# x projected two units ahead, raw token rows in a buffer of their own, expert weights loaded during the last unit, and three shared up-projections at the start of the second stage

## The reference, cut to what matters

```python
def _L0_attn_ref(x, in_proj_w, in_proj_b, conv_w, conv_b, A_log, D, x_proj_w, dt_proj_w, dt_proj_b, out_proj_w, out_proj_b):
    xz = x @ in_proj_w.T + in_proj_b
    x_in, z = jnp.split(xz, 2, axis=-1)
    x_conv = jax.nn.silu(sum((x_pad[:, k:k + L, :] * conv_w[None, None, :, k] for k in range(D_CONV))) + conv_b)
    x_dbl = x_conv @ x_proj_w.T                     # dt_low, B, C
    dt = jax.nn.softplus(dt_low @ dt_proj_w.T + dt_proj_b)
    def step(h, inp):                               # one time step, 512 channels x 16 states
        A_bar = jnp.exp(dtt[..., None] * A)
        B_bar = (A_bar - 1.0) / safe_A * Bt[:, None, :]
        h = A_bar * h + B_bar * xt[..., None]
        return (h, jnp.einsum('bds,bs->bd', h, Ct) + D * xt)
    y = ys * jax.nn.silu(z)
    return y @ out_proj_w.T + out_proj_b
def _L0_ffn_ref(...):                               # 16 experts, top 2, and a shared one
    router_logits = jax.nn.sigmoid(x @ gate_w + gate_b)
    expert_values, expert_indices = jax.lax.top_k(router_logits, k=TOP_K)
    return x + _mlp(x, shared_wg, shared_wu, shared_wd) + expert_weighted
x = _layernorm(x + _L0_attn_ref(...)); x = _layernorm(x + _L0_ffn_ref(...))
```

## Time and profile before

| | |
|---|---|
| median of 3 runs | 2379.16 us (2376.68 to 2380.75) |
| the profiled execution | 2379.85 us, span 2378.0 us |
| first stage, first scan to the barrier | from 56 to 2014.8 us |
| tiles of the experts | 2038.6 to 2280.1 us |
| shared expert and second norm | 2280.1 to 2378.0 us |

### The profile page before, as it was taken

One profiled execution on the slowest core, in us unless ns is written; L12 is line 12 of the kernel. 1 busy time (PEld: TensorE's weight loads), 2 busy tenths in 40 slices (PEclk: granted clock), 3 DMA queues, 4 the chain that ended last, 5 costly groups with the idle time before them and its releaser, 6 DMA issues. The chain is left out here.

```text
span 2378.0 us, 68478 instructions
## 1 busy us (share of the span) xinstructions
PE 2111.4 (89%) x26114; PEld 1270.0 (53%) x26114; DVE 1768.7 (74%) x2992; ACT 1835.2 (77%) x4074; POOL 1772.8 (75%) x1716
## 2 busy tenths in 40 slices
PE   6888989898989898989898989898989878899997
PEld 2454545454555554545455555555545544688864
DVE  2687878787878788787878787878786878555556
ACT  5787888888888879797979797978787875455537
POOL 2688787878686969696969787878787877476654
PEclk8899999999999999999999999999999999899999
DMA  2132333333333323333223232323222333796667
GB/s 92 55 95 89 103 90 95 98 93 93 96 94 93 99 89 96 93 91 92 91 83 99 75 113 79 104 89 100 92 91 93 89 108 98 229 278 213 197 195 265
DMA packets 159218, 269.19 MB, mean 113 GB/s; under 512 B 26536, under 2 KB 74284, under 8 KB 158510
## 3 DMA queue, kind: packets, MB, share of 16 engines
q1 hardware_dynamic: 143294, 220.01, 30.6%
q0 software_dynamic: 15600, 44.79, 5.4%
HBM read 206.27 MB, written 58.45 MB: 111 GB/s over the span
## 5 line engine op out<-in xcount | busy, mean ns | idle before, releaser
L574 POOL TENSOR_TENSOR hc<-h,c_rep 128x512 f32<-128x512 f32 x1024 | 1284.8, 1276 | 369.6 <-DVE h L1129 122.6
L1129 DVE TENSOR_TENSOR_SCAN h<-g_ps,carry,h 128x512 f32<-128x512 f32 x1024 | 1281.5, 1274 | 104.2 <-ACT h L646 79.8
L646 ACT ACTIVATE h<-dt,a_mat 128x512 f32<-128x512 f32 x1024 | 692.0, 712 | 17.4 <-POOL hc L574 16.4
L924 PEld LDWEIGHTS g_ps<-b_steps,x_conv_rows 64*64 64x64 f32 x16384 | 491.5, 137 | 331.4 <-issue 237.5
L924 PE MATMUL g_ps<-b_steps,x_conv_rows 64*64 64x128 f32 x16384 | 569.4, 278 | 74.2 <-DVE h L1129 67.8
L885 PE MATMUL y_ps<-hc,dg_inv 64*64 64x512 f32 x2048 | 525.3, 628 | 23.1 <-POOL hc L574 22.5
L886 PE MATMUL y_ps<-hc,dg_inv 64*64 64x512 f32 x2048 | 523.9, 628 | 0.0
L885 PEld LDWEIGHTS y_ps<-hc,dg_inv 64*64 64x64 f32 x2048 | 141.5, 139 | 261.3 <-issue 168.1
L662 ACT ACTIVATE b_steps<-steps_of,bc_tok 128x64 f32<-128x64 f32 x1024 | 255.9, 341 | 0.0
L1628 POOL DMA_INDIRECT y_planes<-gathered,home x144 | 138.5, 962 | 97.3 <-DVE gathered L2032 74.4
L1120 DVE TENSOR_TENSOR g_ps<-g_ps,minus_u 128x16 f32<-128x16 f32 x512 | 86.8, 170 | 129.8 <-PE g_ps L924 127.2
(11 more groups left out here) (277 smaller groups left out, 2893.1 us busy)
## 6 DMA issues: line engine op xcount, KB each, us to landing
c_rep<-bc_rows SPq DMA_DIRECT2D x512, 256.0 KB
gathered<-slot_rows SPq DMA_DIRECT2D x144, 129.5 KB
gathered<-y_planes SPq DMA_DIRECT2D x32, 512.0 KB, 7.7
x_t<-in_x_t SPq DMA_DIRECT2D x16, 512.0 KB, 3.6
x_tok<-in_x_tok SPq DMA_DIRECT2D x16, 512.0 KB, 4.1
out<-x_t SPq DMA_DIRECT2D x16, 512.0 KB, 2.9
x_t_rows<-y_gated SPq DMA_DIRECT2D x15, 512.0 KB, 3.0
x_t<-x_t_rows POOLq DMA_DIRECT2D x15, 512.0 KB, 5.2
```

The lines of the kernel that those rows point to most:

```text
L574: nc.gpsimd.tensor_tensor(hc[:, at_all % HCS], h[:, at_all % SLOTS], c_rep[:, at % CS], ALU.mult).then_inc(hc_ready, 1)
L646: nc.scalar.activation(h[:, (ITEMS * u + m) % SLOTS], dt[:, c], ACT.Exp, scale=a_mat[:, c, s:s + 1]).then_inc(factor_ready, 1)
L924: one = nc.tensor.matmul(g_ps[some, e, r * T + k * P:r * T + (k + 1) * P], x_rows[rows, c, k, some], steps_of, start=True, stop=True)
L1129: nc.vector.tensor_tensor_scan(slot, du, slot, carry[:, batch(u), c, s:s + 1], ALU.add, ALU.mult).then_inc(scanned, 1)
```

## The change

In the first stage x of unit u+2 is projected at the end of unit u (tiles `X0` to `X3`), where before x of unit u+1 was projected at items 1 and 19 to 26 of unit u; `x0` to `x3` are left for the first unit alone. The buffer `poly` is gone (the softplus works in place in `x_arg`, so `d` tiles wait for `dt_ready` of the chunks before). Four of the eight `make_steps` go from ACT to DVE. The raw rows get their own buffer `x_raw`, loaded when the `o` tiles have been taken; the wait for the scatters goes to DVE's norm sums. Unit 1 scatters nothing any more, and unit 14's rows are scattered by four DMAs behind the last unit and four in the second stage. Most positions in the tables move. `w_in`, `x_t`, `x_conv` lie in the room of `w_up`, which SP fills in four parts during unit 15. In the second stage the bias comes by a matmul, and PE, ACT and DVE make the hidden rows of units 0 to 2 of the shared expert before the expert tiles; LEAD is 6.

```diff
-BY_SCALAR = (0, 1, 2, 3, 4, 5, 6, 7)
+BY_SCALAR = (2, 4, 6, 7)
...
-        NEXT = ["x0", "x1", "x2", "x3", "c0", "c1", "c2", "c3", "low", "bc", "e", "d0", "d1", "a0", "a1", "b0", "b1", "T0", "T1"]
+        FIRST = ["x0", "x1", "x2", "x3"]
+        AFTER_NEXT = ["X0", "X1", "X2", "X3"]
+        NEXT = ["c0", "c1", "c2", "c3", "low", "bc", "e", "d0", "d1", "a0", "a1", "b0", "b1", "T0", "T1"]
...
-        PLACE = [("x0", 1), ("x1", 1), ("d2", 4), ("d3", 4), ("T2", 5), ("T3", 8), ("a2", 11), ("c0", 11), ("c1", 11), ("a3", 15),
+        PLACE = [("x0", 1), ("d2", 1), ("d3", 1), ("x1", 2), ("T2", 4), ("x2", 4), ("c0", 6), ("c1", 6), ("a3", 11), ("T3", 13),
...
-        STEPS_AT = [58, 59, 62, 63, 66, 80, 80, 90]
-        SCATTER_AT = (1, 2, 4, 5, 7, 8, 10, 11)
-        ADD_RELU_AT = (58, 60, 14, 18)
-        Z_AT = (50, 5)
-        SUMS_AT = (19, 20)
+        STEPS_AT = [52, 52, 59, 59, 63, 71, 78, 78]
+        SCATTER_AT = (1, 5, 6, 7, 12, 13, 14, 15)
+        ADD_RELU_AT = (60, 61, 22, 29)
+        Z_AT = (53, 9)
+        SUMS_AT = (20, 21)
...
-        TOKENS_AT, ROWS_OUT_AT, BC_OUT_AT, PARTS_AT = 24, 45, 49, 55
-        C_AT = [4 * (n // 2) + n % 2 + 2 for n in range(2 * QUADS)]
+        TOKENS_AT, ROWS_OUT_AT, BC_OUT_AT, PARTS_AT = 27, 42, 32, 40
+        C_AT = [4 * (n // 2) + n % 2 + -14 for n in range(2 * QUADS)]
...
+        def x_taken(eng, n, some):
+            if n > 0:
+                emptied_all(eng, n - 2, [f"X{c}" for c in some])
+            else:
+                emptied_all(eng, -1, [f"x{c}" for c in some])
...
+            def load_up(n):
+                u = UNITS - 1
+                if n == 0:
+                    emptied_all(sp, u - 1, ["T2", "T3", "r0", "r1", "r2", "r3"])
+                    sp.wait_ge(ends_ready, UNITS)
+                    some = slice(13, NE + 1)
+                elif n == 1:
+                    emptied_all(sp, u, ["d2", "d3"])
+                    some = slice(0, 1)
+                elif n == 2:
+                    emptied_all(sp, u, [f"z{c}" for c in range(CH)])
+                    some = slice(5, 13)
+                else:
+                    emptied_all(sp, u, ["T2", "T3", "r0", "r1", "r2", "r3"])
+                    some = slice(1, 5)
+                sp.dma_start(kept.w_up[:, some], d["w_up"][:, some]).then_inc(up_in, 16)
...
-                    if m == TOKENS_AT and u > 0:
-                        sp.wait_ge(scattered, 16 * 2 * TT * u)
-                        sp.dma_start(x_tok[:], d["x_tok"][u - 1]).then_inc(x_tok_in, 16)
+                    if m == TOKENS_AT and u >= 0:
+                        if u > 0:
+                            emptied_all(sp, u, ["o0", "o1"])
+                        sp.dma_start(x_raw[:], d["x_tok"][u]).then_inc(x_tok_in, 16)
...
-                    if u > 0 and m in SCATTER_AT:
+                    if u > 1 and m in SCATTER_AT:
                         scatter(u, SCATTER_AT.index(m))
+            for n in range(TT):
+                scatter(UNITS, n)
...
-                    if c >= 2:
-                        emptied_all(act, u - 1, ["a0", "a1"])
-                    elif u >= 0:
-                        emptied_all(act, u, ["a2", "a3"])
+                    wait(act, dt_ready, count(own, CH, c // 2 * 2))
...
                 if k == 0:
-                    dve.wait_ge(x_tok_in, count(pu, 16, 32))
+                    dve.wait_ge(x_tok_in, count(pu, 16, 16))
+                    wait(dve, scattered, 16 * 2 * TT * pu)
                 dve.wait_ge(filled[bank], tiles_before(u, t) + 1)
-                two = x_tok[:, 2 * k:2 * k + 2]
-                nc.vector.tensor_tensor(two, work[:, bank].rearrange("p (a b) -> p a b", a=2), two,
+                two = slice(2 * k, 2 * k + 2)
+                nc.vector.tensor_tensor(x_tok[:, two], work[:, bank].rearrange("p (a b) -> p a b", a=2), x_raw[:, two],
                                         ALU.add).then_inc(emptied[bank], 1)
...
-        LEAD = 4
+        LEAD = EARLY_UPS + 3
...
-            sp.dma_start(x_tok[:], d["x_tok"][LAST]).then_inc(x_last_in, 16)
-            sp.dma_start(b_out_rep[:], d["b_out"].to_broadcast([P, DM])).then_inc(x_last_in, 16)
-            sp.dma_start(w_up[:, 0:6], d["w_up"][:, 0:6]).then_inc(experts_in, 16)
-            sp.dma_start(w_up[:, 6:], d["w_up"][:, 6:]).then_inc(experts_in, 16)
+            for i in range(EARLY_UPS):
+                sp.dma_start(x1_t[:, i], d["x1_t"][i]).then_inc(early_x1_t_in[i], 16)
...
-            sp.wait_ge(scattered_before, 16 * 2 * TT)
+            sp.wait_ge(scattered_before, 16 * TT)
...
+            def gate_early(i):
+                act.wait_ge(up_ready, i + 1)
+                nc.scalar.activation(hidden[:, i], early_ps[:, 0], ACT.Silu).then_inc(silu_ready, 1)
+
+            gate_early(0)
             act.wait_ge(norm_step, 4 + 2 * TT)
             nc.scalar.activation(spread[:], spread[:], ACT.Sqrt).then_inc(std_ready, 1)
+            gate_early(1)
...
             def project(tt):
+                nc.tensor.matmul(o_ps[:, tt], kept.full[0:2 * 32 + 1], b_out_parts[:], start=True, stop=False)
...
+            def up_early(i):
+                pe.wait_ge(early_x1_t_in[i], 16)
+                wait(pe, hidden_ready, i)
+                for bank, at in enumerate((0, IF)):
+                    for k in range(KT):
+                        one = nc.tensor.matmul(early_ps[:, bank], w_up[:, SHARED, k, at:at + IF], x1_t[:, i, k], start=(k == 0), stop=(k == KT - 1))
+                one.then_inc(up_ready, 1)
...
-            dve.wait_ge(x_last_in, 2 * 16)
-            V.tensor_tensor(x_tok, x_tok, b_out_rep[:].unsqueeze(1).to_broadcast([P, TT, DM]), ALU.add).then_inc(biased, 1)
-            dve.wait_ge(biased, 1)
+            def gate_early(i):
+                dve.wait_ge(silu_ready, i + 1)
+                V.tensor_tensor(hidden[:, i], hidden[:, i], early_ps[:, 1], ALU.mult).then_inc(hidden_ready, 1)
```

More of the change, by code:

```diff
@@ L769, in halo_out @@
             def halo_out(u):
-                emptied_all(act, u, [f"x{c}" for c in range(CH)])
+                x_taken(act, u + 1, range(CH))
                 act.wait_ge(halo_moved, count(u + 1, 2, 1))
@@ L967, in tile @@
                                               bc_tok[:].rearrange("p k s -> p (k s)"), start=True, stop=True)
[L968 to L970 removed]
+                elif t[0] in "xX":
+                    of = 0 if t[0] == "x" else u + 2
+                    if part == 0:
+                        pe.wait_ge(x_t_in[of % 2], loads(of))
                     m, k = int(t[1]), part
[L972 removed]
+                    mm = nc.tensor.matmul(out, w_in[:, k, m * P:(m + 1) * P], x_t[:, of % 2, k], start=(k == 0), stop=(k == KT - 1))
                 elif t[0] == "z":
@@ L1203, in softplus @@
                 dve.wait_ge(filled[bank], tiles_before(u, t) + 1)
-                if k == 0:
-                    wait(dve, dt_ready, count(n, CH, c - 1))
-                    other = x_arg
-                else:
+                if k == 1:
                     emptied_all(dve, u, [f"a{c}"])
-                    other = poly
-                nc.vector.scalar_tensor_tensor(out=poly[:, c % 2], in0=work[:, bank], scalar=ATANH[k][2], in1=other[:, c % 2],
+                nc.vector.scalar_tensor_tensor(out=x_arg[:, c % 2], in0=work[:, bank], scalar=ATANH[k][2], in1=x_arg[:, c % 2],
                                                op0=ALU.add, op1=ALU.mult).then_inc(emptied[bank], 1)
@@ L1713, in _ @@
             act.wait_ge(made, MADE)
-            for i in range(LEAD):
+            for i in range(EARLY_UPS, LEAD):
                 gate(i)
```

156 lines of the change are left out of this document (84 added, 72 removed), and 8 rows, old and new, of the table PLACE.

## The result

| | before | changed |
|---|---|---|
| median | 2379.62 us | 2253.42 us (2241.39 to 2257.57, 4 runs) |
| profiled execution, span | 2378.0 us | 2239.3 us |

The ratio is 0.9462, 95% interval 0.9428 to 0.9495: 126 us faster, where 77 were forecast (2303, range 2258 to 2350). One execution of `last_scatters_later` took 2657.3 us, with a granted clock of 0.83 over its whole span where its others have 0.97 to 0.98, and is left out.

What follows compares the result with a forecast made beforehand. PE was taken to bound items 9 to 49, ACT and POOL the unit's start and end; -65.0 - 7.0 - 2.0 + 1.0 + 3.5 - 7.5 = -77.0 us from 2379.85 gave 2303, 80% range 2258 to 2350.

Steps and rivals of the forecast that it cites:

- Stretch B: Items 0 to 8 of a middle unit, 18.6 us before: forecast 16.5, with POOL as the bound.
- Stretch A: Items 9 to 49 of a middle unit, bound by PE: from 81.3 us to 75.5, with 1.65 given back for waits.
- Stretches C and D: Items 50 to 58 and 59 to 63: from 13.2 to 15.0 us with PE as bound, and from 9.9 to 11.0.
- Units 0 and 1: First two units: tiles moved out of A free less there, 3.5 us each, -7.0 together.
- the rule against them: New DVE steps and POOL products block each other in SBUF: at most 1.27 us each, 5.1 us a unit.
- The rival: Half of the units' gain lost to DVE steps blocked by POOL or DVE's longer list: 2335 us, chance 0.20.
- The wait for the last scatter: Rival: DVE's norm sums wait for the last scatter, margin 1.4 us; slower, up to 2410 us, chance 0.06.
- The transition: From the units to the second stage's first expert tile: +3.5 us, between +0 and +11.
- The barrier's term: Three column operations and four scatters behind POOL's last product move the barrier from 2014.5 to 2016.4, +1.9 us.
- the 0.8 for the pads: In the transition, DVE zeroing pad rows behind the third product holds the first hidden turn another 0.8 us or so.
- The slow end of the term: In the transition, 10.3 us of matmuls at half clock take up to 10.3 more, making +3.5 up to +11.
- The last stage: Three ups fewer and LEAD 6, less extra mix steps at DVE's pace: -7.5 us, between -4 and -10.3.

Runs made afterwards that it cites:

- last_scatters_later: Changed kernel with all eight scatters of unit 14's rows behind the barrier, at the head of the second stage's POOL list: 2246.8 us, ratio 0.9437.
- before_three_steps_dve: Kernel before with three of the eight make_steps (0, 1 and 5) on DVE, the step at item 63 staying on ACT: 2382.7 us, ratio 1.0015.
- scatters_early: Changed kernel with the eight scatters at items 1, 2, 4, 5, 7, 8, 10, 11, as in the kernel before: 2310.7 us, ratio 0.9714.
- late_c: Changed kernel with SP's loads of repeated C rows 12 items later (offset -2 instead of -14): 2386.5 us, ratio 1.0033.
- before_early_c_tokens: Kernel before with C loads at offset -6 instead of +2 and the raw token load at item 16 instead of 24: 2378.4 us, ratio 0.9997.
- pads_and_scatters: Changed kernel with pad rows zeroed ahead of the third early product and seven of eight scatters one item earlier: 2221.5 us, ratio 0.933.

## Why the prediction was wrong

**What bounds the kernel before.** Right: PE in items 9 to 49, ACT and POOL around the unit's start. before_three_steps_dve bears the second out: with ACT relieved, POOL fills items 59 to 63.

**Stretch B (items 0 to 8), forecast 16.5, measured 14.2.** The failed step is "POOL has nine products ..., four scatters (4.0) ...: 16.5, and POOL is the bound". I counted POOL's work by the items at which it stands in the order. POOL lags DVE by three to five items, so in DVE's stretch it does other work: 13.7 us in fifteen instructions. scatters_early shows that two scatters more do not lengthen the stretch; they are paid at item 11, where PE's sums wait for POOL. What fills the stretch now is DVE, 13.91 of 14.20. I had placed one of DVE's four steps in items 9 to 49; it stands at item 7 and took 1.36 us.

**Stretch A (items 9 to 49), forecast 75.5, measured 72.4.** The failed step is "Since waits that PE's load hid become visible, I give back 1.65". It made PE's waits 5.9 (75.5 less 69.6 of work); they became fewer, 4.2 to 2.6, which makes the error. Two runs bring waits back there: late_c, with POOL held up for C rows, has 7.6 us of them and a stretch of 79.0, scatters_early 4.5 and 76.7. PE's busy time fell by 7.2 against 7.45, but that is in part luck. The granted clock went from 0.98 to 1.00, worth some 1.5 of the 7.2, and the c tiles, counted by their item like POOL's work, mostly did not leave the stretch. PE's 64 c matmuls in unit 9, items 0 to 8, then 9 to 49 (those that lie across a cut are counted on both sides):

```profile
L1036 PE MATMUL work<-room 64*64 64x512 f32 x12 | 1.7, 604 | 0.9 <-ACT x_conv_rows L767 0.9
L1036 PE MATMUL work<-room 64*64 64x512 f32 x56 | 6.6, 588 | 0.0
```

So PE had 11.8 us of work in items 0 to 8 and not 14.3.

**Stretches C and D, forecast 15.0 and 11.0, measured 16.6 and 10.7.** C was 1.6 short: PE worked 16.0 us against my 14.6. The clock, granted at 0.90 there, makes 1.1 of it: units that keep 1.00 have 14.9 of 15.8. D's clock rose to 1.00, as the term assumed. So the sum of the four was 118.0 against 113.9. Of these 4.1 us, 2.8 are waits of PE (the terms leave 118.0 - 109.5 = 8.5, measured 5.7) and 1.3 its work. By stretches, B, A and D were 5.7 too long and C gave 1.6 back.

**The clock** was taken into account in stretch D alone. Of the 8.8 us that a middle unit gained, 6.7 are waits, 1.6 the clock and 0.5 the rest; the forecast held the first at about 4. By stretches the clock's share fell by 1.6 in D, where the forecast had it, and by 1.5 in A, and rose by 1.4 in C: what was missing nearly cancels. Nor is the share always time: in the kernel before, D was filled by ACT (9.81 of 9.9), and before_early_c_tokens has D at 0.71 and A at 1.00 with the same unit of 122.9.

**Units 0 and 1**, forecast -7, measured -19.0. The reason given (less beside them, so the tiles moved out free less) was no reason: unit 0 gained 10.9, more than a middle unit. Which part did it was not tried.

**DVE steps and the rule against them.** A step takes 0.67 us free and 0.95 on the mean in unit 9 (four in 3.7 us), up to 1.36 beside a POOL product (3.04 at most in the whole run); I took 0.62 with ends 0.34 and 1.23. The rival said "at most 1.27 each". That was wrong: the price is the length of POOL's unbroken row (4.83 us above). In unit 9 of the changed kernel POOL has gaps at these places. The Trainium skill's sentence in "SBUF — State Buffer", "Who interferes with whom", that the second to issue is fully blocked, agrees with the trace for DVE (0.67 us became 4.83); the trace adds that POOL's next instructions pass it.

**The wait for the last scatter** was placed right (a margin of 1.4 us) and is there: 2.6 us a unit. It was not free: in pads_and_scatters, where it is 1.0, a unit is 1.6 shorter. As the way to a slower kernel the rival did not come.

**The transition**, forecast +3.5, measured +8.1. The barrier's term failed: 12.0 us behind the last scan and not 6.6 + 1.9 = 8.5. The scatters are at most 1.1 of it, as last_scatters_later shows; the rest is the pause that stays open. From the barrier to the first tile the forecast was +0.8 and the measured +1.9; the 0.8 for the pads is the +0.8 of the expert tiles. The slow end of the term, ups at half clock, is seen in two of the later traces: 4.5 us more before the first tile.

**The last stage**, forecast -7.5, measured -8.0: right.

That the edits are coupled is the other half of the answer. Early C rows cost 125 us in the kernel before, because the token load stands behind them; with a buffer of their own the raw rows no longer depend on the scatters, and C loads twelve items earlier are worth 133 us in the changed kernel. Steps on DVE cost 92 us there and save 76 here. In both cases of C rows the loss came through SP's queue. Summing the edits one by one from the trace of before could not find this.
